# Moving ScalarE's copy of the turned down weight in a hand-written engine order

## The chip, the core and the metric

The kernel runs on one core of one Trainium2 chip. The core has five engines that run side by side, each through its own list of instructions: TensorE (PE in the rows, its weight loads PEld), VectorE (DVE), ScalarE (ACT), GpSimd (POOL) and SyncE (SP, which only starts transfers here). They meet only through semaphores. The metric is device time in microseconds, the median of several executions.

## The reference, cut to what matters

The program is one layer of a language model tower on 16 sequences of 256 tokens, width 256, everything in float32.

```
h = emb_table[ids] @ w1 * mask * 16                 # part A: embedding
h = h + rwkv_block(layernorm(h))                    # parts A and B: time mix, WKV recurrence, channel mix
n = quant(layernorm(h))                             # part C: feed-forward on 4-bit block-quantised operands
gate, y = n @ quant(w_gate).T, n @ quant(w_up).T
h = h + quant(silu(gate) * y) @ quant(w_down).T
```

`quant` scales each block of 16 values by its largest magnitude, rounds to a 4-bit grid and scales back. The weights are quantised once, at the beginning, in the kernel itself.

## The kernel before, in words

The 4096 tokens are cut into 8 chunks of 512 (two sequences, four tiles of 128 tokens). Each chunk goes through three parts: A (gather, embedding, first norm, the k, v and r projections, the recurrence), B (the projection back `b_out`, second norm, the key, gate and value products) and C (norm, quantisation, up and gate products, quantisation, the down product, store). Steps are named by part: `c_cols0` is part C, turning the first pair of quantised tiles into columns. Steps that begin with `w_` prepare weights and run once, for chunk 0. Chunks are numbered from 0 here.

The order in which each engine does its steps is written by hand in the table ORDER: a list of (step, lag) for each engine. The function `walk` runs over a time t and, inside it, over the list, and does each step for chunk t - lag. So the work of neighbouring chunks is interleaved, and in one round of the list TensorE does, for instance, the value product of chunk 0, then `b_out0` of chunk 1, then `c_cols0` of chunk 0. An engine never overtakes in its own list: an instruction whose semaphore isn't there yet holds all that stand behind it.

The down weight w_down is quantised by VectorE, turned (transposed) by TensorE into the PSUM tile psC in `w_turn2` (line 695), and copied from there by ScalarE into `downT` in its own step `w_turn2`. That step has ten instructions on ScalarE: twice three copies (lines 921 to 923), twice a clearing of the unused rows of downT (line 939), and two clearings in hqT (line 943). Six increments of the semaphore s_wd count them (one for each turned half, one for each clearing); TensorE waits for all six at the top of `c_cols0`, since that step writes into the same half of psC:

```
# TensorE, c_cols0 (lines 618 to 631)
                    C.wait_free(pe, ch, f"q{j}")
                    if j == 0:
                        pe.wait_ge(s_wc, 4)
                        pe.wait_ge(s_wd, 6)
                    warm(f"c_cols{j}", ch, psC[:, C.slot(f"q{j}"), 0])
                    at(pe, rounded, ch, ROUNDED * (j + 1))
```

`warm` issues a number of idle transposes of an identity matrix (line 504), for single steps of single chunks by the table WARM. For `c_cols0` of chunk 0 there are 34. They are issued behind the wait for s_wd and ahead of the wait for the rounding of the activations (`rounded`, which VectorE's step `c_rn0` gives at line 1201).

The steps that stand around the change:

- ScalarE, in the order of its list: `b_key3` of chunk 0 (lines 855 and 858), `a_r` of chunk 1 (the sigmoid of r, line 796), `a_wkv3` of chunk 1 (logarithm and exponential, line 820), `a_y` of chunk 1 (line 758), `c_norm0` (873) and `c_sqn0` (897) of chunk 0, `w_turn2`, `c_norm1` (873), `c_cols0` (881, the upper part xq_hi of the columns) of chunk 0, `a_turn0` of chunk 2 (729), `c_sqn1`, `a_emb0` of chunk 2 (742).
- VectorE: `a_wkv3` of chunk 1, `b_value0` and `c_stat0` of chunk 0, `a_wkv4` of chunk 1 (lines 1025 and 1022, which need ScalarE's `a_wkv3`), `c_sn0`, `b_value1`, `c_stat1`, `c_rn0` of chunk 0, `c_sn1` of chunk 0 (1180 to 1186), `b_x1` of chunk 1 (1120, then the statistics 986 and 989), `c_split0` of chunk 0 (1273, the lower part xq_lo of the columns), `c_rn1`.
- TensorE: `b_key3` of chunk 0, `w_turn2` (695), `a_r` (561), `b_value0` (570, with cwv_s), `a_turn0` of chunk 2 (519), `b_value1`, `b_out0` of chunk 1 (570, with wo_s), `c_cols0` of chunk 0 (504, 629), `b_out1` of chunk 1 (570), `a_emb0` of chunk 2 (531), `c_up0` of chunk 0 (645, which waits for VectorE's `c_split0`), `a_turn1` of chunk 2, `c_cols1` of chunk 0, `b_cols` of chunk 1.
- GpSimd: the small coefficients of each norm (452 to 457), the gathers of the embedding rows (444), and the sum `b_sum` (479).

Of the kernel before, what the change touches and what calls it, by code (L numbers as in the profile page):

```python
# [72 lines left out]
    "act": [("w_par", -4), ("c_sq0", 1), ("a_emb1", -1), ("c_up1", 1), ("b_high", 0), ("b_gate", 0),  # L73
        ("c_turn0", 1), ("a_norm", -1), ("w_sq2", 0), ("c_sq1", 1), ("w_sq0", -1), ("c_up2", 1), ("a_cols", -1),
        ("w_key", -1), ("c_turn1", 1), ("b_key0", 0), ("a_part", -1), ("c_sq2", 1), ("c_up3", 1), ("b_key1", 0),
        ("a_k", -1), ("w_turn1", 0), ("b_key2", 0), ("a_wkv1", -1), ("a_v", -1), ("a_wkv2", -1), ("b_key3", 0),
        ("w_turn0", -1), ("c_sq3", 1), ("a_r", -1), ("a_wkv3", -1), ("a_y", -1), ("c_turn2", 1), ("c_norm0", 0),
        ("c_sqn0", 0), ("c_turn3", 1), ("w_turn2", 0), ("c_norm1", 0), ("c_cols0", 0), ("a_turn0", -2),
        ("c_sqn1", 0), ("a_emb0", -2), ("w_sq1", -1), ("c_up0", 0), ("b_norm", -1), ("a_turn1", -2),
        ("c_cols1", 0), ("b_cols", -1), ("b_part", -1)],  # L80
    "dve": [("b_low", 3), ("c_rq1", 4), ("c_up2", 4), ("w_quant0", 2), ("w_quant2", 3), ("c_sq2", 4), ("a_mix", 2),
# [1226 lines left out]
```

## Time and profile before

| | |
|---|---|
| median of 3 executions | 747.94 us (747.89 to 749.3) |
| the profiled execution, its own time | 747.51 us |
| its span, first to last instruction | 745.7 us |
| TensorE busy | 716.9 us (96%) |
| VectorE, ScalarE, GpSimd busy | 589.2 (79%), 510.0 (68%), 154.9 us (21%) |
| mean granted TensorE clock | 0.998 |

The profile records each instruction's start and duration on its engine. "Idle before" is the time for which the engine had nothing running ahead of an instruction, and the arrow behind it names what ended that time. Line numbers (L520) are those of the kernel's file. A share of busy time says how full an engine is, not which wait sets the end: that is read from the stretch itself.

### The profile page before, as it was taken

To read this page: it belongs to the slowest core of one execution; us is meant where nothing else is said; L and a number is where in the kernel's file an instruction comes from. 1 tells how busy PE (TensorE), PEld (TensorE's weight loads), DVE (VectorE), ACT (ScalarE), POOL (GpSimd) and SP (SyncE) were. 2 spreads that over 40 slices of the span, in tenths; PEclk is the share of its full clock that TensorE was granted. 3 is DMA by queue.
4 is the path that set the end of the run, shared out by engine and by line. 5 is a ranking of instruction groups with operands and counts; after the bars stand their busy time and mean duration, and the time that the engine had idled before them with its cause. 6 is when DMAs were issued, how large, how long until landed. Compare 5 with 4: busy or idle time off the path is not lost.

```text
span 745.7 us, 10723 instructions
## 1 busy us (share of the span) xinstructions
PE 716.9 (96%) x3702; PEld 602.9 (81%) x3702; DVE 589.2 (79%) x1031; ACT 510.0 (68%) x893; POOL 154.9 (21%) x220
## 2 busy tenths in 40 slices
PE   6998899899999999999999999999999999899987
PEld 5858767797789968897789868896889878898876
DVE  0687969786988789787998799787998698883685
ACT  2674997488858896589757995689748885663231
POOL 2304401430034201530043201620052002200200
PEclk9999999999999999999999999999999999999999
DMA  4801100100002000100011000100010000000000
GB/s 128 286 2 29 29 0 2 28 30 1 15 9 63 1 1 15 43 29 1 15 41 31 1 1 15 56 16 1 14 43 1 1 14 1 15 1 15 15 1 29
DMA packets 13377, 19.39 MB, mean 26 GB/s; under 512 B 982, under 2 KB 10764, under 8 KB 13324
## 3 DMA queue, kind: packets, MB, share of 16 engines
q1 hardware_dynamic: 10720, 10.31, 4.3%
q0 software_dynamic: 2560, 8.39, 3.8%
q8 instruction: 30, 0.49, 0.3%
q14 instruction: 23, 0.19, 0.1%
q10 hardware_dynamic: 44, 0.01, 0.0%
HBM read 14.51 MB, written 4.19 MB: 25 GB/s over the span
## 4 chain that ended last, share of the span: by engine, by line
PE 78%; DVE 11%; ACT 5%; issue 3%; DMA 1%; POOL 1%; DVEq 0%; ACTq 0%; POOLq 0%
PE psB L570 20%; PE psC L645 15%; PE psB L600 11%; PE psC L672 10%; PE psA L561 9%; PE psA L531 6%; PE psC L660 2%; PE psA L519 1%; PE psC L504 1%; DMA rows<-L_tok_w,ids_now 1%; DVE mix L1000 1%; PE psB L541 1%; DVE mix L1025 1%; PE psC L629 1%; DVE scales L1180 1%
## 5 line engine op out<-in xcount | busy, mean ns | idle before, releaser
L570 PE MATMUL psB<-cwv_s,kkT 128*128 128x256 f32 x512 | 113.2, 379 | 0.7 <-ACT kkT L858 0.7
L570 PEld LDWEIGHTS psB<-cwv_s,kkT 128*128 128x128 f32 x512 | 96.6, 190 | 16.8 <-issue 2.9
L561 PE MATMUL psA<-mix,kvr_s 128*128 128x512 f32 x192 | 86.4, 593 | 3.0 <-DVE mix L1000 1.8
L645 PE MATMUL psC<-up_hi,xq_hi 128*128 128x352 f32 x256 | 85.9, 335 | 2.1 <-DVE xq_lo L1273 1.5
L452 POOL TENSOR_SCALAR sc_c<-mv_c 128x2 f32<-128x2 f32 x16 | 7.6, 474 | 384.7 <-DVE mv_c L1163 384.7
L672 PE MATMUL psC<-downT,hqT 128*128 128x256 f32 x384 | 85.9, 380 | 0.1
L645 PE MATMUL psC<-up_hi,xq_lo 128*128 128x352 f32 x256 | 82.6, 323 | 0.0
L645 PE MATMUL psC<-up_lo,xq_hi 128*128 128x352 f32 x256 | 82.5, 322 | 0.0
L672 PEld LDWEIGHTS psC<-downT,hqT 128*128 128x128 f32 x384 | 72.2, 190 | 10.3 <-ACT hqT L923 0.5
L561 PEld LDWEIGHTS psA<-mix,kvr_s 128*128 128x128 f32 x192 | 36.1, 190 | 40.3 <-issue 36.3
L1000 DVE SCALAR_TENSOR_TENSOR mix<-hT,rest,mix 128x512 f32<-128x512 f32 x80 | 54.5, 748 | 16.3 <-ACT mix L774 16.3
L531 PE MATMUL psA<-w_s,rowsT 128*128 128x256 f32 x256 | 57.9, 379 | 0.0
L600 PE MATMUL psB<-key_hi,cwk_hi 128*128 128x512 f32 x128 | 56.4, 440 | 0.9 <-ACT kkT L855 0.5
L531 PEld LDWEIGHTS psA<-w_s,rowsT 128*128 128x128 f32 x256 | 47.9, 190 | 6.1
L645 PEld LDWEIGHTS psC<-up_hi,xq_hi 128*128 128x128 f32 x256 | 48.1, 188 | 5.7 <-DVE xq_lo L1273 4.1
L774 ACT ACTIVATE mix<-hT,par 128x512 f32<-128x512 f32 x80 | 50.9, 724 | 0.9
L600 PE MATMUL psB<-key_lo,cwk_hi 128*128 128x512 f32 x128 | 50.6, 396 | 0.0
L600 PE MATMUL psB<-key_hi,cwk_lo 128*128 128x512 f32 x128 | 50.6, 395 | 0.0
L645 PEld LDWEIGHTS psC<-up_hi,xq_lo 128*128 128x128 f32 x256 | 48.1, 188 | 0.2
L645 PEld LDWEIGHTS psC<-up_lo,xq_hi 128*128 128x128 f32 x256 | 48.1, 188 | 0.0
L444 POOL DMA_INDIRECT rows<-L_tok_w,ids_now x32 | 36.1, 1128 | 44.5 <-PE psA L519 29.5
L873 ACT ACTIVATE normc<-h,sc_c 128x256 f32<-128x256 f32 x32 | 17.5, 593 | 39.0 <-POOL sc_c L457 39.0
(170 smaller groups left out, 1561.6 us busy)
## 6 DMA issues: line engine op xcount, KB each, us to landing
out<-h SPq DMA_DIRECT2D x16, 256.0 KB, 2.1
mix<-L_attn_cwk SPq DMA_DIRECT2D x1, 1024.0 KB, 10.4
cwv_s<-L_attn_cwv SPq DMA_DIRECT2D x1, 1024.0 KB, 13.2
hq<-L_ffn_w_gate SPq DMA_DIRECT2D x1, 704.0 KB
hq<-L_ffn_w_up SPq DMA_DIRECT2D x1, 704.0 KB, 6.7
hqT<-L_ffn_w_down SPq DMA_DIRECT2D x1, 704.0 KB, 10.2
w_s<-L_tok_w SPq DMA_DIRECT2D x1, 512.0 KB, 3.6
rows<-L_tok_w,ids_now POOLq DMA_INDIRECT x32, 4.0
```

The source lines that it names most:

```text
L444: pool.indirect_dma_start(rows[:, q, :], None, tok_w0, bass.IndirectOffsetOnAxis(ap=ids_now[:, s, t:t + 1], axis=0)).then_inc(rows_in[q], 16)
L452: nc.gpsimd.tensor_scalar(sc[:, 0], mv[:, :, 1], EPS, None, ALU.add).then_inc(coef.sem, 1)
L531: mm = nc.tensor.matmul(psA[:, A.slot(f"e{j}"), q * D:(q + 1) * D], rowsT[:, q, k, :], w1_s[:, k, :], start=(k == 0), stop=(k == KE - 1))
L561: mm = nc.tensor.matmul(psA[:, A.slot(f"{name}{d}")], kvr_s[:, w, k, d * P:(d + 1) * P], mix[:, w, k].rearrange("p c t -> p (c t)"), start ...
L570: mm = nc.tensor.matmul(psB[:, B.slot(name), q * D:(q + 1) * D], lhsT[:, k, (2 * j + q) * P:(2 * j + q + 1) * P], weight[:, k, :], start=( ...
L600: mm = nc.tensor.matmul(psB[:, B.slot(f"kk{m}")], a[:, k, m * P:(m + 1) * P], b[:, k], start=(k == 0 and p == 0), stop=(k == H - 1 and p = ...
L645: mm = nc.tensor.matmul(psC[:, C.slot(name), f, 0:INTER // 2], a[:, k, t * P:(t + 1) * P], b[:, w, k, f * (INTER // 2):(f + 1) * (INTER // ...
L660: mm = nc.tensor.transpose(psC[0:n, C.slot(name), k // 4, (k % 4) * P:(k % 4 + 1) * P], hq[:, t, k * P:k * P + n], ident[:])
L672: mm = nc.tensor.matmul(psC[:, C.slot(name), 0, q * D:(q + 1) * D], hqT[:, q, k, :], downT[:, k, :], start=(k == 0), stop=(k == KI - 1))
L774: nc.scalar.activation(dst[:, w, d], src[:, d, :, 1:ROW], ACT.Identity, scale=col(m, d)).then_inc(sig.sem, 1)
L873: nc.scalar.activation(normc[:, t, :], h1[:, ch.parity, t, :], ACT.Identity, scale=sc_c[:, 1, t:t + 1], bias=sc_c[:, 3, t:t + 1]).then_inc ...
L1000: nc.vector.scalar_tensor_tensor(out=dst[:, w, d], in0=src[:, d, :, 0:T], scalar=rest[:, PARAMS.index(m) - MIXES, d:d + 1], in1=dst[:, w, ...
```

## The change

In ScalarE's list the step `w_turn2` is moved: it stood behind `c_turn3` (nothing for a chunk that doesn't exist yet) and `c_sqn0` of chunk 0, and it now stands directly behind `b_key3` of chunk 0. No other list is touched; the instructions of the step, its semaphores and TensorE's waits are the same.

```
     "act": [("w_par", -4), ("c_sq0", 1), ...
...
-        ("a_k", -1), ("w_turn1", 0), ("b_key2", 0), ("a_wkv1", -1), ("a_v", -1), ("a_wkv2", -1), ("b_key3", 0),
+        ("a_k", -1), ("w_turn1", 0), ("b_key2", 0), ("a_wkv1", -1), ("a_v", -1), ("a_wkv2", -1), ("b_key3", 0), ("w_turn2", 0),
         ("w_turn0", -1), ("c_sq3", 1), ("a_r", -1), ("a_wkv3", -1), ("a_y", -1), ("c_turn2", 1), ("c_norm0", 0),
-        ("c_sqn0", 0), ("c_turn3", 1), ("w_turn2", 0), ("c_norm1", 0), ("c_cols0", 0), ("a_turn0", -2),
+        ("c_sqn0", 0), ("c_turn3", 1), ("c_norm1", 0), ("c_cols0", 0), ("a_turn0", -2),
```

Steps passed by the move that do something in this round: `a_r`, `a_wkv3` and `a_y` of chunk 1, `c_norm0` and `c_sqn0` of chunk 0.

## Rows read from the trace of the kernel before

**Rows 1.** Windows: length, busy (x) of PE, PEld, DVE, ACT, POOL; clock, DMA, GB/s

```profile
0.00:160.00 160.00, 140.56 (x787) 115.68 (x788) 113.83 (x208) 105.24 (x182) 43.14 (x66) 0.99 0.20 62
160.00:620.00 460.00, 460.00 (x2267) 384.02 (x2266) 387.36 (x678) 352.38 (x613) 97.40 (x133) 1.00 0.06 17
```

**Rows 2.** Who waited for whom on TensorE: us in total, times, longest

```profile
PE psC L504 <- ACT hqT L943: 3.3, 1, 3.3
```

**Rows 3.** Timeline of TensorE, 109 to 147 us: start, duration, instructions

```profile
109.98 1.47 PE L695 MATMUL psC<-ident,hqT 128*128 128x128 f32 x12
...
122.60 1.04 PE L519 MATMUL psA<-ident,rows 128*128 128x128 f32 x8
...
130.48 1.97 PE L570 MATMUL psB<-wo_s,rT 128*128 128x256 f32 x8
135.73 5.56 PE L504 MATMUL psC<-ident 128*128 128x128 f32 x34 [3.29 <-ACT hqT L943]
141.13 0.60 PE L629 MATMUL psC<-ident,normc 128*128 128x128 f32 x4
141.57 1.89 PE L570 MATMUL psB<-wo_s,rT 128*128 128x256 f32 x8
143.30 3.62 PE L531 MATMUL psA<-w_s,rowsT 128*128 128x256 f32 x16
146.68 0.40 PE L645 MATMUL psC<-up_hi,xq_hi 128*128 128x352 f32 x1
```

**Rows 4.** TensorE's granted clock (third number from the right) in short stretches

```profile
80.00:84.00 4.00, 2.65 (x13) 1.00 0.21 70
...
136.00:139.00 3.00, 3.00 (x16) 0.50 0.00 0
139.00:140.00 1.00, 1.00 (x10) 0.92 0.10 29
```

**Rows 5.** Timeline of ScalarE, 114 to 143 us

```profile
114.39 1.14 ACT L858 ACTIVATE kkT<-kkT 128x512 f32<-128x512 f32 x2
115.55 1.28 ACT L796 ACT_TABLE_LOAD   x1
...
120.89 1.23 ACT L820 ACTIVATE take<-keep 128x512 f32<-128x512 f32 x2 [1.66 <-DVE keep L1025]
...
123.44 1.15 ACT L820 ACTIVATE take<-take 128x512 f32<-128x512 f32 x2
...
128.50 1.09 ACT L873 ACTIVATE normc<-h,sc_c 128x256 f32<-128x256 f32 x2 [1.95 <-POOL sc_c L457]
...
132.72 0.57 ACT L921 COPY downT<-psC 128x512 f32<-128x512 f32 x1
...
135.10 0.49 ACT L943 ACTIVATE hqT<-ident 64x128 f32<-64x128 f32 x2
137.54 1.09 ACT L873 ACTIVATE normc<-h,sc_c 128x256 f32<-128x256 f32 x2 [1.95 <-POOL sc_c L457]
...
142.31 1.08 ACT L729 COPY rowsT<-psA 128x512 f32<-128x512 f32 x2
```

**Rows 6.** Timeline of VectorE, 125 to 147 us

```profile
125.35 1.26 DVE L1025 TENSOR_TENSOR mix<-keep,take 128x512 f32<-128x512 f32 x2
...
135.97 0.69 DVE L1201 SCALAR_TENSOR_TENSOR normc<-normc,scales 128x512 f32<-128x512 f32 x1
138.66 0.69 DVE L1180 TENSOR_REDUCE scales<-normc 128x32 f32<-128x512 f32 x1 [2.00 <-ACT normc L873]
...
140.60 0.68 DVE L1120 TENSOR_TENSOR mix<-psB,takev 128x512 f32<-128x512 f32 x1
143.50 0.69 DVE L1120 TENSOR_TENSOR mix<-psB,takev 128x512 f32<-128x512 f32 x1 [2.22 <-PE psB L570]
...
145.89 0.69 DVE L1273 TENSOR_TENSOR xq_lo<-psC,xq_hi 128x512 fp32r<-128x512 f32 x1
```

**Rows 7.** Timeline of GpSimd, 144 us

```profile
144.28 2.34 POOL L479 TENSOR_TENSOR h<-h,mix 128x1024 f32<-128x1024 f32 x1 [3.85 <-DVE mix L1120]
```

## The prediction, as it went on record

> **What bounds the kernel now.** I read the windows first. Between 160 and 620 us TensorE is busy for all of the 460 us at a granted clock of 1.00, while VectorE is busy for 387 us of them and ScalarE for 352 [rows 1]. So the long middle is TensorE's own work back to back. Nothing that ScalarE does earlier can shorten it; it can only begin sooner. The first 160 us hold 140.6 us of TensorE's work, so some 19 us of idle time are there, and this is where the moved step lies. What is gained before 160 us reaches the end in full, since a block without a gap behind it moves as a whole; the tail from 620 us on depends only on that block.
>
> The waits of TensorE come second. The longest of a single kind but for one at the very start is 3.3 us, once: the idle transposes of L504 on ScalarE's last clearing of hqT, L943 [rows 2]. That is the wait for s_wd at the top of `c_cols0`, and L943 is the last instruction of the step that the change moves.
>
> The timeline then shows what this wait costs. TensorE starts `b_out0` at 130.48 and ends it at 132.45, stands still, and starts its 34 idle transposes at 135.73 [rows 3]. ScalarE's step runs from 132.72 to 135.10 + 0.49 = 135.59 [rows 5], 0.14 us ahead of that start. The transposes themselves that the step copies were there since 109.98 + 1.47 = 111.45 [rows 3]. So the data waits for 21 us, and TensorE for 3.3.
>
> There is a second cost. From 136 to 139 us the clock is 0.50, that is 1.2 instead of 2.4 GHz, and back at 1.00 (0.92 over the whole microsecond) from 139 on [rows 4]. The engine had stood still for 3.3 us before it fell. The 34 transposes take 141.13 - 135.73 = 5.40 us [rows 3]: the 16 that lie in the low stretch of 3.00 us take 0.19 to 0.22 us each [rows 4], and the four of L629 at the full clock 141.57 - 141.13 = 0.44, so 0.11 us each [rows 3]. At the full clock 34 would take 3.7 us.
>
> **The change, part by part.** *What it adds and removes.* No instruction. The ten of `w_turn2` keep their kind, and no DMA hangs on them.
>
> *The step in its new place.* ScalarE ends the squares of `b_key3` at 114.39 + 1.14 = 115.53 and goes on at once with a table load for `a_r` [rows 5]. The data is there since 111.45, so the step doesn't wait: there are 4.1 us to spare. It takes 135.59 - 132.72 = 2.87 us [rows 5], so it ends at 118.40, and TensorE has its s_wd 12 us before it asks for it.
>
> *What stands behind it on ScalarE.* `a_r` and `a_wkv3` of chunk 1 start up to 2.87 us later. I follow each until a gap takes it up.
> - r is written 2.87 us later, by about 120.8. TensorE's next use of that PSUM is `a_turn0` of chunk 2 at 122.60 [rows 3], so nothing is late.
> - The logarithm started at 120.89 after 1.66 us of idle time in which it waited for VectorE [rows 5]. Of the 2.87 us, 1.66 go there, and 1.2 stay. The two exponentials that ended at about 124.05 and at 123.44 + 1.15 = 124.59 [rows 5] now end at 125.25 and 125.8.
> - VectorE takes them in `a_wkv4`, at 125.35 and, half of the 1.26 us pair later, at about 125.95 [rows 6]. It is busy until then with `c_stat0`. So both are still there in time, by 0.10 and 0.15 us. This cover is thin: with it gone each further microsecond passes straight into VectorE's chain, which is the next to matter. I take the cost as 0 and, from a semaphore's way of 0.14 us (above), its upper bound as 0.3 us.
> - `a_y` is 1.2 us later, and `c_norm0` at 128.50 had 1.95 us of idle time before it, waiting for GpSimd [rows 5]. Covered, with 0.75 to spare. So `c_norm0` and `c_sqn0` stay where they were, and so does `c_rn0`.
>
> *What the old place gives back.* Behind the step stood `c_norm1`. It didn't start at 135.6 but at 137.54, after 1.95 us in which it waited for GpSimd's coefficients [rows 5]. These come from VectorE's `c_stat1`, which the change doesn't touch. So `c_norm1` gains nothing and stays at 137.54 to 138.63. This decides how much of TensorE's gain survives.
>
> *TensorE.* `b_out0` keeps its place. The idle transposes start right behind it, at about 132.2 instead of 135.73, 3.5 us sooner. With the clock still at 1.00 they end at 132.2 + 3.7 = 135.9, with it low at 137.6. `c_cols0` needs `c_rn0` too, which ends at 135.97 + 0.69 = 136.66 [rows 6]. So it starts at 136.75 rather than 141.13, 4.4 us sooner (3.5 with the low clock), and `b_out1` at 137.2, ending by 139.1.
>
> *Where this is given back.* `c_up0` needs VectorE's xq_lo, L1273, and that stands behind `c_sn1` and `b_x1` in VectorE's list. `c_sn1` begins at 138.66, when `c_norm1` is done, and the first half of `b_x1` follows at 140.60 [rows 6]; both stay. The second half waited 2.22 us for `b_out1`, until 143.50 [rows 6]. Now `b_out1` is done at 139.1 (140.0 with the low clock), before VectorE comes, so the second half starts at 140.60 + 0.7 = 141.3. It moves by 2.2 us and no more, whatever TensorE does. L1273 stands 145.89 - 143.50 = 2.39 us behind it [rows 6]: it runs from 143.7 to 144.4. Before it ended at 146.58, and `c_up0` started at 146.68 [rows 3], so now at 144.45 to 144.5.
>
> TensorE's `a_emb0` between them needs rowsT, which ScalarE writes behind `c_norm1` and xq_hi: it was written from 142.31 on [rows 5], 1.2 us behind the start of `c_cols0`; now xq_hi follows `c_norm1` at 138.6 and rowsT comes from 139.1 to 140.1. `a_emb0` runs from 139.7 to 143.1 (its distance to `c_up0`, 146.68 - 143.30 = 3.4 us, [rows 3]) and is no hindrance; TensorE waits 1.3 us ahead of `c_up0`.
>
> *The others at this point.* GpSimd's `b_sum` started at 144.28, 3.85 us after its last work, on the second half of `b_x1` [rows 7]. It moves by the same 2.2 us, and with it the coefficients and the norm that `b_cols` needs; its gathers, whose issues lie before this, stay, and `a_turn1` asks for them 5 us later. So all four engines move together from here.
>
> *Sum.* 146.68 - 144.48 = 2.2 us. Of TensorE's 3.3 us of idle time and 1.7 us of slow transposes, 5.0 in all, 2.8 us come back as three short waits. The profiled execution would go from 747.51 to 745.3. It lies 0.4 us below the median, so I forecast a median of 747.94 - 2.2 = 745.7 us, 0.3% less.
>
> *A rule against it.* The Trainium skill (ScalarE: Activation LUTs, "What ACT_TABLE_LOAD costs") prices a switch to another set of tables at 1.28 us for the load and 1.38 us for a drain. In the row the load takes 1.28 us and starts 0.02 us behind the squares [rows 5], so no drain is seen there. The same page ("Table sets: the hidden batching unit") says that cheap functions such as copy are in every set. By that the moved copies need no load, and the sum stays; if they needed one the page would have it cost 2.66 us instead of the row's 1.28, and the gain would be gone.
>
> **The rivals.**
> - *The thin cover breaks* (less faster). If ScalarE's block is slower between the squares and the sigmoid, by a table load of 1.28 us [rows 5] or by copies that take longer next to other work, VectorE's `a_wkv4` is late by what exceeds 0.1 to 0.15 us, and the whole of VectorE's chain up to L1273 with it. For it: the margin is small. Against it: the copies ran at the old place without a load ahead of them. With one load the gain is 2.2 - 1.15 = 1.05 us: 746.9. With tenths only, 746.1.
> - *The clock falls later on* (nearly the same). TensorE now has waits of 0.7, 0.6 and 1.3 us where it had one of 3.3. If the clock falls behind them, 3.4 us of work at half speed cost 1.7 us, as the idle transposes did. Ahead of 141 us that would hide in the wait before `c_up0`; behind it the gain shrinks to 0.5 us: 747.4. Against it: from 80 to 84 us TensorE was busy for 2.65 of 4 us and the clock was 1.00 [rows 4].
> - *No change.* If `c_up0` were set by something that I hold to be moved along, by the norm for `b_cols` or by a gather, the shift would be taken up behind 146.68: 747.9. The idle transposes' wait would be gone, and the waits behind it longer by as much.
> - *Slower.* ScalarE stands at the head of its list at 115.5 for the turned weight. If TensorE's transposes came late, `a_r`, `a_wkv3` and everything behind would be held, where before they passed. The point from which this counts is 4.1 us later than now; the cover of 0.15 and the gain of 2.2 are used up at 6.4 us, and from 8 us on it is slower by over 1.5 us: 749.4. Against it: nothing ahead of L695 is changed, so 111.45 should stand.
>
> **How the numbers follow.** The forecast gets 0.74, the broken cover 0.09 (tenths 0.06, a load 0.03), the low clock 0.07, no change 0.06, slower 0.04. About 0.2% (1.5 us) is what a measurement of this kernel tells from no change; its three executions before lay 1.4 us apart. Faster by over 0.2% means below 746.4: the forecast, and most of the tenths, 0.78. Within 0.2%: 0.18. Slower: 0.04. For the range I take 0.3 us of extra gain and 0.3 us of measuring below 745.7, so 745.1, and above it the broken cover with a load, 746.9 to 747.0. Outside lie the low clock, no change and slower, 0.17 together.
>
> **What the profile after would show.** L921 first at 115.5 and L943 ending at 118.4; the sigmoid's table load behind it; the logarithm at about 122.1 with no idle time before it; `a_wkv4` still at 125.35. TensorE's wait for L943 gone, L504 at 132.2 and lasting 3.7 us with a clock of 1.00 throughout; L629 at 136.75, waiting for L1201; L1120's second half directly behind its first at 141.3; L645 at 144.5 after 1.3 us, now released by VectorE's L1273; then every row of TensorE 2.2 us sooner until the end. It would be wrong if L1025 of `a_wkv4` waited for ScalarE, if a low clock showed after 141 us, or if the stretch of TensorE without idle time began as late as before.

## The result and the profile after

The changed kernel takes 746.75 us in the median of 7 executions (745.66 to 747.08), the kernel before 749.3 us in 7 taken beside it (747.76 to 749.45). The ratio is 0.9973, with a 95% interval of 0.9962 to 0.9984: 0.27% faster, 2.0 us. The two medians themselves lie 2.55 us apart: the times of both kernels lie on two levels, as is shown below, and a median picks one execution of the mixture. Forecast were 0.30% (2.2 us) and 745.7 us, with a range of 745.1 to 747.0. Two executions of the kernel before, run beside the experiments, took 1495 and 2618 us and are left out everywhere.

The profiled execution of the changed kernel took 746.75 us, with a span of 744.9 us. That is only 0.8 us under the span of before. To see where the rest is, one has to begin at the far left. The sixteen matmuls of `a_emb1` in the kernel before:

```profile
18.68 3.62 PE L531 MATMUL psA<-w_s,rowsT 128*128 128x256 f32 x16
```

and TensorE's rows of the same microseconds in the changed kernel:

```profile
16.72 0.65 PE L519 MATMUL psA<-ident,rows 128*128 128x128 f32 x4 [1.49 <-DMA rows<-L_tok_w,ids_now]
17.90 0.66 PE L519 MATMUL psA<-ident,rows 128*128 128x128 f32 x4 [0.53 <-DMA rows<-L_tok_w,ids_now]
18.39 5.31 PE L531 MATMUL psA<-w_s,rowsT 128*128 128x256 f32 x16
```

They take 5.31 us here instead of 3.62. The clock of the changed kernel in windows says why. A row gives start:end, the length, TensorE's busy time with its count of matmuls in brackets, and then the granted clock (0.77, 0.50, 0.52):

```profile
18.00:19.00 1.00, 1.00 (x6) 0.77 0.01 4
19.00:21.00 2.00, 2.00 (x6) 0.50 0.79 230
21.00:22.00 1.00, 1.00 (x4) 0.52 1.19 315
```

The clock fell to half at about 18.5 us, and in the execution of before that was profiled it didn't (1.00 from 18 to 24 us). The transposes of w_down stood at 109.98 there [rows 3] and stand at 111.40 here: everything behind is 1.42 us later from the start, in code that the change doesn't touch. The other traces bear this out: `w_turn2` (L695) starts at 111.40 to 111.77 us in the three in which the clock fell at 18 us (the changed kernel, e5 and e12), and at 109.96 to 110.34 us in the eleven in which it didn't. So the two traces have to be laid over each other at L695, and I take 1.42 us off below.

The stretch of the change on TensorE, answering to [rows 3]:

```profile
111.40 1.47 PE L695 MATMUL psC<-ident,hqT 128*128 128x128 f32 x12
...
133.72 3.88 PE L504 MATMUL psC<-ident 128*128 128x128 f32 x34
138.15 0.66 PE L629 MATMUL psC<-ident,normc 128*128 128x128 f32 x4 [0.56 <-DVE normc L1201]
138.64 1.89 PE L570 MATMUL psB<-wo_s,rT 128*128 128x256 f32 x8
141.16 3.69 PE L531 MATMUL psA<-w_s,rowsT 128*128 128x256 f32 x16 [0.63 <-ACT rowsT L729]
145.80 0.40 PE L645 MATMUL psC<-up_hi,xq_hi 128*128 128x352 f32 x1 [0.95 <-DVE xq_lo L1273]
```

The wait of 3.29 us for L943 is gone, the 34 idle transposes take 3.88 us instead of 5.56, and three short waits of 0.56, 0.63 and 0.95 us stand in their place: for L1201, for rowsT and for L1273. From L695 to the first matmul of `c_up0` it is now 145.80 - 111.40 = 34.40 us; before it was 146.68 - 109.98 = 36.70 [rows 3]. The change is worth 2.30 us at this point. Behind it TensorE is as full as before, here in the windows by engine (busy time of PE, PEld, DVE, ACT, POOL, then the clock, as in [rows 1]):

```profile
0.00:160.00 160.00, 141.43 (x792) 115.44 (x793) 114.58 (x209) 105.58 (x182) 43.19 (x66) 0.99 0.20 62
160.00:620.00 460.00, 460.00 (x2266) 383.97 (x2265) 387.26 (x679) 352.81 (x613) 97.49 (x133) 1.00 0.06 17
```

GpSimd's `b_sum` (L479) starts at 143.40 - 1.42 = 141.98 where it started at 144.28 [rows 7], 2.30 us sooner as well. So nothing is given back later: 745.7 + 1.42 - 2.30 = 744.8, against a measured span of 744.9 us.

ScalarE, answering to [rows 5]:

```profile
115.83 1.14 ACT L858 ACTIVATE kkT<-kkT 128x512 f32<-128x512 f32 x2
116.87 0.57 ACT L921 COPY downT<-psC 128x512 f32<-128x512 f32 x1
...
119.26 0.49 ACT L943 ACTIVATE hqT<-ident 64x128 f32<-64x128 f32 x2
119.77 1.28 ACT L796 ACT_TABLE_LOAD   x1
...
125.93 1.15 ACT L820 ACTIVATE take<-take 128x512 f32<-128x512 f32 x2
...
129.94 1.09 ACT L873 ACTIVATE normc<-h,sc_c 128x256 f32<-128x256 f32 x2 [0.90 <-POOL sc_c L457]
...
138.97 1.09 ACT L873 ACTIVATE normc<-h,sc_c 128x256 f32<-128x256 f32 x2 [4.72 <-POOL sc_c L457]
```

The step runs directly behind the squares, waits for nothing and needs no table load of its own. `c_norm0` comes at 129.94 - 1.42 = 128.52 and `c_norm1` at 137.55, where they were. The wait ahead of `c_norm1` has grown from 1.95 to 4.72 us: the place that the step left is simply empty. VectorE, answering to [rows 6]:

```profile
126.78 1.26 DVE L1025 TENSOR_TENSOR mix<-keep,take 128x512 f32<-128x512 f32 x2
...
137.40 0.69 DVE L1201 SCALAR_TENSOR_TENSOR normc<-normc,scales 128x512 f32<-128x512 f32 x1
140.10 0.69 DVE L1180 TENSOR_REDUCE scales<-normc 128x32 f32<-128x512 f32 x1 [2.00 <-ACT normc L873]
...
142.03 1.28 DVE L1120 TENSOR_TENSOR mix<-psB,takev 128x512 f32<-128x512 f32 x2
...
145.01 0.69 DVE L1273 TENSOR_TENSOR xq_lo<-psC,xq_hi 128x512 fp32r<-128x512 f32 x1
```

`a_wkv4` comes at 125.36 and without a wait, so the thin cover held. Both halves of `b_x1` (L1120) now stand as one pair without a gap, and L1273 comes at 143.59 instead of 145.89 [rows 6].

### The profile page after: what moved, and what is told of

The parts are those of the page before. It is cut to its first block, busy times and chain, and to the rows that moved or that the text cites. A ratio compares the mean times of both kernels' runs of the same rounds, so it can differ in the third digit from the quotient of the medians.

```text
span 744.9 us, 10723 instructions
## 1 busy us (share of the span) xinstructions
PE 716.9 (96%) x3702; PEld 601.9 (81%) x3702; DVE 589.1 (79%) x1031; ACT 510.0 (68%) x893; POOL 155.1 (21%) x220
## 4 chain that ended last, share of the span: by engine, by line
PE 76%; DVE 12%; ACT 5%; issue 4%; DMA 1%; POOL 1%; DVEq 0%; ACTq 0%; POOLq 0%
PE psB L570 19%; PE psC L645 15%; PE psB L600 11%; PE psC L672 10%; PE psA L561 9%; PE psA L531 6%; PE psC L660 2%; PE psA L519 1%; DVE mix L1000 1%; DMA rows<-L_tok_w,ids_now 1%; PE psB L541 1%; DVE mix L1025 1%; DVE scales L1180 1%; PE psC L629 1%; PE psA L541 1%
## 5 line engine op out<-in xcount | busy, mean ns | idle before, releaser
L531 PE MATMUL psA<-w_s,rowsT 128*128 128x256 f32 x256 | 59.6, 387 | 0.6 <-ACT rowsT L729 0.6
```

Of the source, the lines that this page charges most:

```text
L531: mm = nc.tensor.matmul(psA[:, A.slot(f"e{j}"), q * D:(q + 1) * D], rowsT[:, q, k, :], w1_s[:, k, :], start=(k == 0), stop=(k == KE - 1))
```

## The experiments

Two questions were open. What was the harm in the old order: the wait itself, or the 34 idle transposes that ran behind it at half clock? And where do the 1.4 us at the start come from? Each ratio is to the kernel before, run on the same chip; the chips differ between groups of experiments, so ratios and distances are compared below, not medians. "L695 to c_up0" is the distance used above: 36.70 us before, 34.40 after.

**e1: the old order without the 34 idle transposes.**

```
# kernel before
-        ("b_cols", 0): 33, ("c_cols0", 0): 34, ("c_up0", 6): 32, ...
+        ("b_cols", 0): 33, ("c_up0", 6): 32, ...
```

> The kernel before, in its old order, with the 34 idle transposes ahead of c_cols0 of chunk 0 left out. Theory (the gain is cut by VectorE's chain c_norm1, c_sn1, b_x1, c_split0; the slow idle transposes behind the wait, not the wait itself, were what held that chain): c_cols0 starts when c_rn0 is done, 4.3 us sooner, at half clock; b_out1 still ends before VectorE comes for it; c_up0 starts about 2.2 us sooner and the time falls by about 2.0 to 2.2 us, as much as by the change. Rival (the wait of 3.3 us for s_wd is what the change gained, the clock only a by-product): the clock stays low into c_up0 and little is gained, 0 to 0.5 us. Rival (the idle transposes are needed): 1 to 2 us slower than before.

Measured: ratio 0.9975 (0.9963 to 0.9987), median 746.83 us. The profiled execution took 745.42 us, with a span of 743.6 us (745.7 before) and its mean clock at 0.998 as in that of before. TensorE:

```profile
109.96 1.47 PE L695 MATMUL psC<-ident,hqT 128*128 128x128 f32 x12
...
136.81 1.09 PE L629 MATMUL psC<-ident,normc 128*128 128x128 f32 x4 [4.36 <-DVE normc L1201]
137.69 2.87 PE L570 MATMUL psB<-wo_s,rT 128*128 128x256 f32 x8
140.39 3.62 PE L531 MATMUL psA<-w_s,rowsT 128*128 128x256 f32 x16
144.38 0.40 PE L645 MATMUL psC<-up_hi,xq_hi 128*128 128x352 f32 x1 [0.37 <-DVE xq_lo L1273]
```

its clock in windows:

```profile
136.00:137.00 1.00, 0.19 (x1) 0.62 0.00 0
137.00:139.00 2.00, 2.00 (x8) 0.50 0.00 0
139.00:140.00 1.00, 1.00 (x5) 0.67 0.03 4
```

and VectorE:

```profile
140.61 1.28 DVE L1120 TENSOR_TENSOR mix<-psB,takev 128x512 f32<-128x512 f32 x2
...
143.58 0.69 DVE L1273 TENSOR_TENSOR xq_lo<-psC,xq_hi 128x512 fp32r<-128x512 f32 x1
```

TensorE stands still for 4.36 us, longer than ever, and its clock falls: `b_out1` takes 2.87 us instead of 1.89. Still L695 to c_up0 is 34.42 us, the same as in the changed kernel to 0.02 us. VectorE's chain is the one of the changed kernel: both halves of `b_x1` in one pair and L1273 at 143.58. The wait was harmless without the idle transposes behind it, even at 4.36 us, and so was the low clock, since TensorE has to wait for L1273 in any case. What did the harm was 5.4 us of idle transposes behind the wait. The rival that the wait was the cost has fallen, and so has the one that the idle transposes are needed.

**e2: the new order without them.** The same edit in the changed kernel.

> The changed kernel with the same 34 idle transposes left out. TensorE then stands still for some 4.4 us ahead of c_cols0 and its clock should fall. Theory: about 3.4 us at half clock cost 1.7 us of TensorE's time, but most of them lie ahead of c_up0, where TensorE waits 1.0 to 1.3 us for VectorE anyway; the time stays within 0.5 us of the changed kernel. Rival (the clock matters as such): 1.5 to 1.7 us slower than the changed kernel, so 0.5 to 0.8 us faster than before.

Measured: ratio 0.9965 (0.9953 to 0.9977), median 746.22; L695 to c_up0 34.40 us. The clock fell here too, behind 4.37 us without work, and TensorE still waited 0.34 us for L1273. With or without idle transposes, in the new order and (without them) in the old one, `c_up0` comes at the same time.

**e9: the old order with 24 of them instead of 34.**

> The kernel before, in its old order, with 24 idle transposes ahead of c_cols0 of chunk 0 instead of 34. Theory (what counts is when b_out1 is done against VectorE's coming for it at 141.3 on the scale of the kernel before): where the clock falls, the 24 end at 135.73 + 3.4 + 8 x 0.11 = 140.0, b_out1 some 2.3 us behind it at 142.3, so 1.0 of the 2.2 us is still lost: 1.1 us faster than before, half of what leaving all out gives. Rival (any idle transposes behind the wait cost the full 2.2 us, or none unless all 34 are there): the time of before, or that of the changed kernel.

Measured: ratio 0.9988 (0.9979 to 0.9997), median 747.32. TensorE:

```profile
110.03 1.47 PE L695 MATMUL psC<-ident,hqT 128*128 128x128 f32 x12
...
135.79 4.48 PE L504 MATMUL psC<-ident 128*128 128x128 f32 x24 [3.29 <-ACT hqT L943]
140.10 0.60 PE L629 MATMUL psC<-ident,normc 128*128 128x128 f32 x4
...
145.65 0.40 PE L645 MATMUL psC<-up_hi,xq_hi 128*128 128x352 f32 x1
```

L695 to c_up0 is 35.62 us, 1.08 less than before where 1.0 to 1.1 was expected. The ratio of the times says the same, 0.9 us, though its interval ends just below 1. With 34, 24 and none of them the distance is 36.70, 35.62 and 34.42 us: the cost grows with the length of the idle work, and both rivals have fallen.

**e10: four more copies in the moved step.** They go into parts of hq that are free at that time. The same copies into a spare tile of their own (e7) have no result, since SBUF had no room for that tile.

```
# changed kernel, ScalarE, w_turn2
+                            for e in range(2):
+                                nc.scalar.copy(hq[:, 2 * d + e, 0:512], psC[:, d, 0])
                             turned(psC, d, downT[:, :, d * P:(d + 1) * P], s_wd)
```

> The changed kernel with four more copies of 128 x 512 from the same PSUM inside w_turn2, into parts of hq that are written anew before they are read: 0.48 to 0.57 us each, 2.0 us in all. Theory (the cover behind the step on VectorE is 0.1 to 0.15 us): the exponentials and with them a_wkv4 on VectorE are late by about 1.85 us, and all of VectorE's chain up to c_split0 with them: 1.85 us slower than the changed kernel, 0.3 us faster than before. Rival (VectorE or ScalarE has more room behind): less than 1 us slower than the changed kernel.

Measured: ratio 0.9993 (0.9984 to 1.0001), median 747.4, so the times alone can't tell it from the kernel before. Among the executions with a mean clock of 0.999 or 1.00 the median span is 745.5 us, 1.7 us above that of the changed kernel (743.8). On VectorE (two lines further down in this file, so L1027 is L1025), with L695 at 110.34:

```profile
127.46 1.29 DVE L1027 TENSOR_TENSOR mix<-keep,take 128x512 f32<-128x512 f32 x2 [1.65 <-ACT take L820]
```

`a_wkv4` now waits 1.65 us for ScalarE's exponential. L695 to c_up0 is 36.16 us, 1.76 more than in the changed kernel, for 1.93 us of added work on ScalarE (the step and its copies run from 115.81 to 120.61, 4.80 us, against 2.87 [rows 5]). So the cover was 0.17 us, where the prediction had 0.10 and 0.15.

**e5: the step behind a_y instead.**

```
# changed kernel
-        ... ("b_key3", 0), ("w_turn2", 0),
+        ... ("b_key3", 0),
-        ... ("a_y", -1), ("c_turn2", 1), ("c_norm0", 0),
+        ... ("a_y", -1), ("w_turn2", 0), ("c_turn2", 1), ("c_norm0", 0),
```

> The changed kernel with ScalarE's w_turn2 three steps later: behind a_y of chunk 1, ahead of c_norm0. Theory: a_wkv3 isn't delayed at all, s_wd comes about 129.4 on the scale of the kernel before, still ahead of TensorE at 132.2; of the 2.87 us 1.95 lie in ScalarE's wait for GpSimd, and c_norm0 and with it VectorE's chain is late by 0.9 us less what VectorE's own backlog hides (c_sn0 began 0.5 us after c_norm0 was done): 0.3 to 0.5 us of the 2.2 us gain are lost. Rival (any place ahead of TensorE's wait is as good): no loss against the changed kernel.

Measured: ratio 0.9964 (0.9952 to 0.9976), median 746.06. L695 to c_up0 is 146.50 - 111.77 = 34.73 us, 0.33 more than in the changed kernel: the expected size, seen in the trace of one execution but too small for the times. In the trace the wait for L1201 has grown from 0.56 to 0.91 us, by 0.35.

**e6: the step one place sooner, ahead of b_key3.**

```
# changed kernel
-        ("b_key3", 0), ("w_turn2", 0),
+        ("w_turn2", 0), ("b_key3", 0),
```

> The changed kernel with w_turn2 one step sooner on ScalarE, ahead of b_key3 of chunk 0. Theory: the step waits for nothing or for some tenths, but the squares of b_key3 end 2.8 us later, b_value0 on TensorE waits for them, and TensorE and VectorE's chain move by about 2.8 us: about 2.8 us slower than the changed kernel, 0.6 us slower than before. Rival (TensorE catches up in its later waits of 0.6 and 1.0 us): 1.0 to 1.5 us slower than the changed kernel, still faster than before.

Measured: ratio 1.0033 (1.0023 to 1.0044), median 751.28, so 2.5 us slower than before. TensorE, with L695 at 110.12:

```profile
118.79 8.81 PE L570 MATMUL psB<-cwv_s,kkT 128*128 128x256 f32 x32 [3.76 <-ACT kkT L858]
```

and its clock in windows:

```profile
118.00:119.00 1.00, 0.21 (x1) 0.86 0.00 0
119.00:122.00 3.00, 3.00 (x8) 0.50 0.02 5
```

The squares hold `b_value0` by 3.05 us, about as expected (2.8). What I missed is the clock: behind 3.76 us without work the 32 matmuls run for 8.81 us instead of the 7.17 that the same form takes in the changed kernel. L695 to c_up0 is 39.08 us, 4.68 more than in the changed kernel: 3.05 of delay and 1.64 of slow matmuls. Here nothing hides the slow stretch, since VectorE's chain hangs on `b_value0`. In e1 something did.

**e8: c_split0 ahead of b_x1 on VectorE.**

```
# changed kernel, "dve"
-        ... ("c_sn1", 3), ("b_x1", 2), ("c_split0", 3), ...
+        ... ("c_sn1", 3), ("c_split0", 3), ("b_x1", 2), ...
```

> The changed kernel with VectorE's c_split0 ahead of b_x1 in every round. Theory (c_up0 waits for L1273 alone, 1.0 us, after a_emb0): in the first round c_up0 starts 1.0 us sooner, right behind a_emb0; but b_x1, b_sum, the coefficients and the norm that b_cols waits for come 0.7 us later, so TensorE waits there, and in the sum 0 to 0.7 us are lost in that round. Rival (L1273 was the only limit): 1.0 us faster than the changed kernel.

Measured: ratio 1.0035 (1.0022 to 1.0048), median 751.43. L695 to c_up0 falls to 33.10 us, 1.3 us better. But in the waits of TensorE there is now:

```profile
PE psB L541 <- issue: 7.7, 7, 2.3
```

In the changed kernel that wait is 0.8 us, once. L541 is `b_cols`. The trace names no releaser ("issue"); by the kernel's code `b_cols` waits there for the norm behind `b_x1`, so the cause is argued from the code and not read from the trace. The time was lost not only in the first round but in seven, since a list holds for all rounds: against the changed kernel the ratios give 4.6 us, where 0 to 0.7 us were expected for one round.

**e3 and e4: twelve idle transposes in the wait at 15 us,** in the old and in the new order.

```
+        ("a_turn1", 0): 12,
```

> The kernel before with 12 more idle transposes of 0.11 to 0.22 us ahead of a_turn1 of chunk 0, in the wait of 1.5 to 1.95 us for the gathered rows at 15 to 17 us. Theory of the two levels (a fall of TensorE's clock at 18.5 us, which the changed kernel's profiled execution has and that of before has not, costs 1.4 us in some executions of any kernel): all executions near 747.8 us, and the clock 1.00 from 18 to 22 us. Rival (the two levels come from elsewhere): still two groups 1.4 us apart. Second rival: the transposes end after the rows have come and cost up to 1 us each time.

> The changed kernel with the same 12 idle transposes ahead of a_turn1 of chunk 0. Theory: all executions near 745.7 us, none near 746.9, so 2.1 us less than the kernel before with the same addition, which is the change's worth without the scatter of the two levels. Rival (the change made the fall of the clock more frequent): the scatter remains in this one.

Measured, e4: five executions of 745.64 to 745.85 us with mean clocks of 1.00 (one 0.999), ratio 0.9956 (0.9943 to 0.9969). e3: eleven of 746.27 to 750.0 us, median 747.94, ratio 0.9991 (0.9982 to 1.0). Between the two orders with the same addition lie 2.2 us. In e3 two of the eleven still have a mean clock of 0.995 and spans of 747.0 and 748.2 us, as if a second fall had come in spite of the twelve. No trace of these two was kept, so it isn't known where it lay. The profiled execution of e3 shows something that I hadn't expected:

```profile
110.21 1.47 PE L695 MATMUL psC<-ident,hqT 128*128 128x128 f32 x12
...
135.97 3.90 PE L504 MATMUL psC<-ident 128*128 128x128 f32 x34 [3.29 <-ACT hqT L943]
139.72 0.60 PE L629 MATMUL psC<-ident,normc 128*128 128x128 f32 x4
...
145.26 0.40 PE L645 MATMUL psC<-up_hi,xq_hi 128*128 128x352 f32 x1
```

and its clock there:

```profile
136.00:139.00 3.00, 3.00 (x28) 1.00 0.00 0
```

The old order, the same wait of 3.29 us, and yet the clock stays at 1.00: the 34 take 3.90 us. L695 to c_up0 is 35.05 us. So where the clock doesn't fall, the old order costs 0.65 us against the new, and where it falls 2.30 us. 1.65 of the change's 2.30 us need both things together, the idle transposes and the fall of the clock under them; e1 shows the fall without the transposes, which costs nothing. The spans agree (744.5 us in this execution, 743.9 in that of e4), but it is one execution: the single one of the kernel before with a mean clock of 1.00 has a span of 745.5 us, and why it isn't shorter is open.

**e12 and e13: the changed kernel again, and with 16 early idle transposes.**

> The changed kernel itself beside the next one, for the share of executions in which TensorE's clock falls at 18.5 us. Theory (each execution draws for itself): some with mean clock 1.00 and a span of 743.8 to 744.1 us, some with 0.998 and 744.9 to 745.3 us, none between.

> The changed kernel with 16 idle transposes instead of 12 ahead of a_turn1 of chunk 0: 16 x 0.109 = 1.75 us from 15.3 to 17.0 us, the whole of the wait for the rows. Theory (the early fall of the clock comes from TensorE's waits at 15 to 17 us): all executions with mean clock 1.00 and spans of 743.8 to 744.2 us, at most 0.2 us more where the rows come before the transposes end. Rival (the early fall has another cause and the five even executions of the kernel with 12 were luck): some at 745.0 us again.

Measured, e12: 745.08, 745.24 and 745.61 us with clocks of 0.999 and 1.00, 746.6 and 746.84 with 0.998; ratio 0.9963 (0.9949 to 0.9977). e13: five of 745.11 to 745.55 us, all 0.999 or 1.00; ratio 0.9958 (0.9945 to 0.9972). TensorE in e13, with `a_emb1` at full speed:

```profile
15.05 1.91 PE L504 MATMUL psB<-ident 128*128 128x128 f32 x16
16.80 0.60 PE L519 MATMUL psA<-ident,rows 128*128 128x128 f32 x4
18.25 0.66 PE L519 MATMUL psA<-ident,rows 128*128 128x128 f32 x4 [0.86 <-DMA rows<-L_tok_w,ids_now]
18.75 3.62 PE L531 MATMUL psA<-w_s,rowsT 128*128 128x256 f32 x16
```

None of ten executions of e4 and e13 has the upper level; six of the twelve of the changed kernel have it (the seven of the result and the five of e12), and so have about half of the kernel before, 30 of 63. So nothing shows that the change makes it more frequent. That idle transposes in the wait at 15 to 17 us keep the early fall away is likely by this, not settled: the two odd ones of e3 may speak against a full cure. e13 is the best version found, 745.23 us in the median.

**e11: c_stat1 ahead of c_sn0 on VectorE,** with the twelve early ones.

```
# changed kernel, "dve"
-        ("a_wkv4", 2), ("c_sn0", 3), ("b_value1", 3), ("w_split0", 2), ("c_stat1", 3), ("c_rn0", 3),
+        ("a_wkv4", 2), ("b_value1", 3), ("w_split0", 2), ("c_stat1", 3), ("c_sn0", 3), ("c_rn0", 3),
```

> The changed kernel with the 12 early idle transposes and with b_value1 and c_stat1 ahead of c_sn0 in VectorE's list. Theory (VectorE's chain from c_norm1 to c_split0 is the last limit of the first round): c_norm1 comes 1.9 us sooner, c_sn1, b_x1 and c_split0 1.1 us sooner, c_up0 starts right behind a_emb0: up to 1.0 us faster than the changed kernel with the early transposes, 744.7 us. Rival (in the later rounds c_rn0, now 0.8 us later, holds c_cols0, as the reorder of c_split0 held b_cols): as much or more lost, 745.8 to 750 us.

Measured: ratio 1.0309 (1.0276 to 1.0341), median 770.24. L695 to c_up0 is 33.68 us, 0.7 better in the first round, as the chain says. In the waits of TensorE:

```profile
PE psC L672 <- ACT hqT L923: 20.1, 7, 2.9
```

The down product waits for its turned operand in each of seven rounds. The clock also fell at several later places (mean 0.991). The loss is far more than expected (up to 750 us); through which of the lists it comes isn't shown.

## Why the prediction was right in its mechanism, and where it was off

- *"The step in its new place ... doesn't wait":* right. It ends at 119.75 - 1.42 = 118.33, forecast 118.40.
- *"Both are still there in time, by 0.10 and 0.15 us":* right. e10 measured the cover as 0.17 us and showed that all beyond passes straight through.
- *"`c_norm1` gains nothing and stays":* right, at 137.55 against 137.54.
- *"`c_cols0` starts at 136.75":* 136.73. The 34 idle transposes ran at full clock, ending by 136.2.
- *"TensorE now has waits of 0.7, 0.6 and 1.3 us":* right in number and place; they are at 0.56, 0.63 and 0.95 us in the trace, each behind the modelled end of the work ahead of it.
- *"It moves by 2.2 us and no more, whatever TensorE does":* right. L1273 moved by 2.30, `c_up0` from 146.68 to 144.38 where 144.48 was forecast. In e1 and e2, where TensorE did much else, L695 to `c_up0` is the same to 0.02 us.
- *"All four engines move together from here":* right, `b_sum` moved by 2.30 us too and no new wait came behind.
- *The low clock as a rival, hidden ahead of 141 us:* no fall was seen in this stretch; the one that came lay far ahead of it, see below. Where e1 forced one, it was hidden indeed.
- *"Nothing ahead of L695 is changed, so 111.45 should stand"* and *"It lies 0.4 us below the median, so I forecast a median of 747.94 - 2.2 = 745.7":* this is the step that failed. The code ahead of L695 was unchanged and yet L695 ended at 112.87 in the profiled execution: the clock fell at 18.5 us, a term of 1.4 us that the sum put at nothing. The prediction subtracted its 2.2 us from a median of three as if all executions lay on one level, and took the 1.4 us between those three for scatter. They lie on two levels. 63 executions of the kernel before that ran beside the experiments have a mean clock of 0.997 or 0.998 in 32 (median span 746.0 us), 0.995 or less in 30 (747.4 us), and 1.00 in one. Of the changed kernel's twelve, the five with 0.999 or 1.00 have spans of 743.3 to 743.9 us, six of the seven with 0.998 have 744.8 to 745.3, and one has 744.1. In both traces of the changed kernel (its own and e12), and in that of e5, the mean clock is 0.998 and the one fall is that at 18 us. The mean alone doesn't say where a fall lies: in e8, also at 0.998, it is at 645 to 655 us. For the kernel before no trace of an execution with 0.995 was kept, so that its upper level is the same fall is inferred from the clock and the distance of 1.4 us.
- So 745.7 us was a forecast of the lower level, and the three executions near it took 745.66 to 745.89 us. The other four took 746.75 to 747.08, and the median fell among them, 1.05 us above the forecast. The medians of before, 747.94 and then 749.3, were two draws from the same mixture. Level against level the change is worth 746.0 - 743.8 = 2.2 us and 747.4 - 745.0 = 2.4 us, as forecast. That the median of seven still lies between 745.1 and 747.0 is luck: the upper end of that range stood for a broken cover, which didn't happen.
- The prediction did speak of the clock, as the "second cost" of 1.7 us, but took its fall as given. e3 shows an execution without it, in which the change's worth is 0.65 us. Only one of 63 executions of before has a mean clock of 1.00, so the fall came nearly always, and the sum could do without that distinction. It was luck that it could.

## What to carry to other kernels

Look on which side of a wait the idle work stands that is put in to keep the clock up. Here 34 idle transposes stood behind a semaphore wait and were ordinary work on the path: they cost 2.3 us where the clock had fallen and 0.65 us where it hadn't, and leaving them out brought as much as moving ScalarE's step. Ahead of the wait that they fill, in the new order, they cost nothing (34.40 us with and without them). When a wait goes, look for the engine that comes next in the chain and read off when it could have started; that, not the length of the wait, is the gain. And before two traces are subtracted, lay them over each other at an instruction ahead of the change: executions of one program can differ there by as much as the change is worth.

## What the runs showed of the hardware

- TensorE's clock fell behind a wait of 3.29 us in the profile of before and not behind the same wait of 3.29 us in that of e3. The same idle time doesn't decide it alone.
- It also fell at 18.5 us behind waits of only 1.49 and 0.53 us in the changed kernel, while in the kernel before, in the same code, waits of 1.95 and 0.40 us left it at 1.00, and in e2 even nearly the same ones (1.52 and 0.63 us). In three of the ten traces without additional early transposes it fell there, in none of the four with them.
- Each fall lasted about 3.4 us. This is the sum of length times the missing share of the clock, doubled, over the windows: in the changed kernel 0.46 + 2.00 + 0.96 = 3.42 us, in e1 0.76 + 2.00 + 0.66 = 3.42 us. It cost 1.4 us (the early one) to 1.65 us (the idle transposes and, in e6, `b_value0`), and nothing in e1 and e2, where another wait stood behind to hide it.
